# Loading a tile's rows from ScalarE's queue, and 159 tiles instead of 160, in a mixture-of-experts stage

## The reference

```python
B, S, H = (2, 512, 512)
E, G, TKG, K = (32, 8, 4, 8)
I, SI = (256, 512)
...
flat_idx = top_k_index.reshape(-1)
sort_idx = jnp.argsort(flat_idx)
xs = jnp.repeat(x, K, axis=0)[sort_idx]
group_sizes = jnp.bincount(flat_idx, length=E).astype(jnp.int32)
gate = jax.lax.ragged_dot(xs, w_gate, group_sizes)
up = jax.lax.ragged_dot(xs, w_up, group_sizes)
down = jax.lax.ragged_dot(jax.nn.silu(gate) * up, w_down, group_sizes)
unsort = jnp.argsort(sort_idx)
routed = (down[unsort].reshape(T, K, H) * tkw[..., None]).sum(axis=1)
```

## Time and profile before

| | |
|---|---|
| Median of 3 runs | 3160.15 us (3156.3 to 3161.93) |
| The profiled execution's own time | 3153.92 us |
| Its span, first to last instruction | 3151.8 us |
| Stage `expert_stage1` within it | about 2139 to 3152 us |
| TensorE clock granted, mean of the span | 0.961 of full speed |

### The profile page before, as it was taken

The page is one execution under the profiler, slowest core; times in us unless marked ns, Lnnn a source line. Parts: engine busy times, 40 slices in busy tenths (PEclk is TensorE's granted clock), DMA queues, the critical chain, the costliest instruction groups (busy, mean ns, idle before and its releaser), DMA issues. The chain is left out here.

```text
span 3151.8 us, 34237 instructions
## 1 busy us (share of the span) xinstructions
PE 2793.4 (89%) x9573; PEld 1264.9 (40%) x9574; DVE 1425.5 (45%) x2593; ACT 775.0 (25%) x1192; POOL 1211.3 (38%) x866
## 2 busy tenths in 40 slices
PE   5987975899999887689889988977999999999997
PEld 2343431344444343233333333433444454444453
DVE  7999999322000232376675646212332333232332
ACT  4746643200000010134333422001111111111111
POOL 2777656033000221154545321772333333333332
PEclk8999999999999998899999998988999999999999
DMA  3333221311200699730672002655656555756544
GB/s 123 118 101 101 81 66 48 111 55 56 71 14 38 230 354 327 200 100 1 170 196 68 1 1 92 262 223 147 149 125 147 127 130 129 182 127 149 125 89 72
DMA packets 270850, 386.49 MB, mean 123 GB/s; under 512 B 48546, under 2 KB 165091, under 8 KB 270754
## 3 DMA queue, kind: packets, MB, share of 16 engines
q1 hardware_dynamic: 212434, 243.23, 24.5%
q0 software_dynamic: 58320, 142.02, 19.1%
HBM read 237.38 MB, written 160.53 MB: 126 GB/s over the span
## 5 line engine op out<-in xcount | busy, mean ns | idle before, releaser
L1919 PE MATMUL e_psg<-e_wgu,e_xsT 128*128 x1280 | 592.7, 606 | 13.9 <-issue 8.9
L1799 POOL DMA_INDIRECT out_x<-e_yo,e_dest x160 | 255.7, 1598 | 637.5 <-DMA out_x<-e_yo,e_dest 452.9
L282 POOL TENSOR_TENSOR hc<-hs,bcst 128x1024 f32<-128x1024 f32 x128 | 300.6, 2349 | 178.4 <-DVE ps_b L502 171.4
L1919 PEld LDWEIGHTS e_psg<-e_wgu,e_xsT 128*128 128x128 f32 x1280 | 232.8, 192 | 258.5 <-issue 257.5
L627 PE MATMUL ps_y<-hc,ident 128*128 128x512 f32 x512 | 241.1, 609 | 90.4 <-POOL hc L282 90.1
L1868 DVE TENSOR_TENSOR e_h<-e_psg,e_sg 128x256 f32<-128x256 f32 x160 | 68.0, 425 | 530.4 <-ACT e_sg L1828 530.4
L1935 PE MATMUL e_pso<-e_wd,e_hT 128*128 x640 | 300.8, 592 | 0.7 <-DVE e_hT L1863 0.7
L508 DVE TENSOR_TENSOR_SCAN hs<-dA,ps_b 128x1024 f32<-128x1024 f32 x128 | 292.7, 2286 | 7.0 <-ACT dA L412 2.7
L1828 ACT ACTIVATE e_sg<-e_psg 128x256 f32<-128x256 f32 x160 | 61.3, 383 | 650.5 <-PE e_psg L1919 650.5
L1182 PE MATMUL r_ps_t<-r_wd,r_h 128*128 128x512 f32 x480 | 210.9, 600 | 10.3 <-issue 5.2
L412 ACT ACTIVATE dA<-dt,a_neg 128x511 f32<-128x511 f32 x256 | 165.6, 713 | 111.8 <-DVE hs L508 106.7
(11 more groups left out here) (404 smaller groups left out, 3861.7 us busy)
## 6 DMA issues: line engine op xcount, KB each, us to landing
e_xs<-slots_in POOLq DMA_DIRECT2D x160, 272.0 KB, 4.9
slots_in<-zeros SPq DMA_DIRECT2D x160, 256.0 KB, 2.3
bcst<-bc_rows SPq DMA_DIRECT2D x128, 256.0 KB, 4.3
e_wgu<-in_wg SPq DMA_DIRECT2D x32, 512.0 KB, 5.8
e_wgu<-in_wu SPq DMA_DIRECT2D x32, 512.0 KB, 7.0
e_wd<-in_wd SPq DMA_DIRECT2D x32, 512.0 KB, 7.9
e_w<-in_wg SPq DMA_DIRECT2D x11, 1408.0 KB, 15.5
e_w<-in_wu SPq DMA_DIRECT2D x11, 1408.0 KB, 16.8
```

What stands on the lines that cost most here:

```text
L282: pool.tensor_tensor(hc[:, it % 2, half(h), :], hs[:, it % 2, half(h), :], bc(bcst[:, q, 1, :], 1, HB), ALU.mult).then_inc(sem["hc"], 1)
L1799: pool.indirect_dma_start(out[:, :], bass.IndirectOffsetOnAxis(dest[:, q, 0:1], 0), yo[:, q, :], None, bounds_check=T + P - 1, oob_is_err= ...
L1919: j = pe.matmul(ps_g[:, q % 2, :], xsT[:, q % 2, k, :], wgu[:, bass.ds(e % RING, 1), k, :], start=k == 0, stop=k == KH - 1)
```

## The change

Three things change, all in or around `expert_stage1`.

1. The four first loads and all later ones (`load`, `reload`) move from POOL's program to ACT's. On ACT, `reload(t-1)` stands between `gate(t)` and `empty(t-1)`; on POOL only the adds are left.
2. `NTILE1` is worked out as (16384 + 32 x 127) // 128 = 159 instead of 16384 / 128 + 32 = 160. The slots in DRAM still number 160 x 128.
3. The last round of the loops has three tiles instead of four, and ACT's last round stands outside its loop.

```diff
-NTILE1 = T * K1 // P + E
-NSLOT1 = NTILE1 * P
+NTILE1 = (T * K1 + E * (P - 1)) // P
+NSLOT1 = (NTILE1 + 1) * P
...
-                def load(t, q):
-                    pool.dma_start(xs[:, q, :], D["xs1"][bass.ds(t * P, P), :]).then_inc(rows_in[q], 16)
...
-                def reload(t, q):
-                    hold(pool, sem["tr"], 1 + t + 1, c["held"])
-                    hold(pool, sem["dest"], 1 + t + 1, c["held"])
-                    load(t + RING, q)
...
                 with pool.Fori(1, ROUNDS - 1) as i:
                     for q in range(RING):
-                        reload(i * RING + q, q)
                         add(i * RING + q, q)
...
+                def load(t, q):
+                    act.dma_start(xs[:, q % RING, :], D["xs1"][bass.ds(t * P, P), :]).then_inc(rows_in[q % RING], 16)
+
+                def reload(t, q):
+                    hold(act, sem["tr"], 1 + t + 1, c["held"])
+                    hold(act, sem["dest"], 1 + t + 1, c["held"])
+                    load(t + RING, q)
...
-                with act.Fori(2, ROUNDS) as i:
+                with act.Fori(2, ROUNDS - 1) as i:
                     for q in range(RING):
                         gate(i * RING + q, q)
+                        reload(i * RING + q - 1, q + RING - 1)
                         empty(i * RING + q - 1, q + RING - 1)
```

More of the change, by code:

```diff
@@ L1730, in expert_stage1 @@
         RING = RING1
-        assert NTILE1 % RING == 0 and E % RING == 0
+        assert E % RING == 0
         assert AHEAD == RING - 1
@@ L1757, in expert_stage1 @@
         sem["out"] = pl.sem0("e1_out")
-        ROUNDS = NTILE1 // RING
+        ROUNDS = -(-NTILE1 // RING)
+        LAST = NTILE1 - (ROUNDS - 1) * RING
+        assert 1 < LAST < RING
         pl.start_at_one()
@@ L1801, in add @@
                         .then_inc(sem["out"], 16)
-                def reload(t, q):
-                    hold(pool, sem["tr"], 1 + t + 1, c["held"])
-                    hold(pool, sem["dest"], 1 + t + 1, c["held"])
-                    load(t + RING, q)
-                for q in range(RING):
-                    load(q, q)
-                reload(0, 0)
                 add(0, 0, first=True)
                 for q in range(1, RING):
-                    reload(q, q)
                     add(q, q)
@@ L1816, in _ @@
                     for q in range(RING):
-                        reload(i * RING + q, q)
                         add(i * RING + q, q)
-                for q in range(RING):
-                    add(NTILE1 - RING + q, q)
+                for t in range((ROUNDS - 1) * RING, NTILE1):
+                    add(t, t % RING)
                 pool.wait_ge(sem["out"], 16 * NTILE1)
@@ L1836, in empty @@
                        .then_inc(sem["yo"], 1)
+                def load(t, q):
[4 more added lines that the diff above has]
+                    load(t + RING, q)
+                for q in range(RING):
+                    load(q, q)
                 for t in range(RING):
@@ L1840, in _ @@
                     if t > 0:
+                        reload(t - 1, t - 1)
                         empty(t - 1, t - 1, first=True)
                 gate(RING, 0)
+                reload(RING - 1, RING - 1)
                 empty(RING - 1, RING - 1, first=True)
@@ L1845, in _ @@
                     gate(RING + q, q)
+                    reload(RING + q - 1, q - 1)
                     empty(RING + q - 1, q - 1)
-                with act.Fori(2, ROUNDS) as i:
+                with act.Fori(2, ROUNDS - 1) as i:
                     for q in range(RING):
                         gate(i * RING + q, q)
+                        reload(i * RING + q - 1, q + RING - 1)
                         empty(i * RING + q - 1, q + RING - 1)
-                empty(NTILE1 - 1, RING - 1)
+                for q in range(LAST):
+                    gate((ROUNDS - 1) * RING + q, q)
+                    if (ROUNDS - 1) * RING + q - 1 + RING < NTILE1:
+                        reload((ROUNDS - 1) * RING + q - 1, q + RING - 1)
+                    empty((ROUNDS - 1) * RING + q - 1, q + RING - 1)
+                empty(NTILE1 - 1, LAST - 1)
             @block.vector
@@ L1884, in a_round @@
                 def a_round(i, first=False, last=False):
-                    for q in range(RING):
+                    for q in range(LAST if last else RING):
                         t = i * RING + q
-                        if not (last and q == RING - 1):
+                        if not (last and q == LAST - 1):
                             turned_rows(t + 1, q + 1)
@@ L1903, in _ @@
                 a_round(ROUNDS - 1, last=True)
-                turned_hidden(NTILE1 - 1, RING - 1)
+                turned_hidden(NTILE1 - 1, LAST - 1)
             @block.tensor
@@ L1956, in _ @@
                 a_round(ROUNDS - 1, last=True)
-                turn_hidden(NTILE1 - 1, RING - 1)
-                down(NTILE1 - 1, RING - 1)
+                turn_hidden(NTILE1 - 1, LAST - 1)
+                down(NTILE1 - 1, LAST - 1)
 def attention_stage(nc, c, I, D, x, A, ln1, wr1, bias1):
```

## The result

The change ran in 3135.16 us (median of 4 executions, 3131.83 to 3141.76), the kernel before in 3159.53 us beside it: ratio 0.9933, 95% interval 0.9919 to 0.9948, 24.4 us faster. The forecast was 3165 us. Of the rivals, B with 3141 us came nearest. The profiled execution of the change is its slowest, 3141.76 us with a span of 3140.0; that of the kernel before is its fastest, so the two profiles lie only 11.8 us apart.

What follows compares the result with a forecast made beforehand. Adds were taken to bound the first stretch, PE the last. Terms -5.8 - 5 - 7 - 1 + 24 gave +5 us onto 3153.92, 3159; with the median 6 us above the profiled execution, 3165 us, range 3125 to 3195.

Steps and rivals of the forecast that it cites:

- B: Rival, faster: loads slip between the adds and cost them nothing; 3141 us, mostly 3125 to 3145; chance 0.30.
- What bounds the kernel: Last stage: adds, one at a time, pace the first stretch at 6.23 us, PE the second at 5.93 us.
- One tile, -5.8: Last stage: one padding tile fewer saves a quiet step of 5.68 to 5.93 us, taken as -5.8 us.
- Late rows, -5: First stretch: moving loads off POOL ends PE's 10.0 us of waits for rows; worth -5 us, between 0 and 10.0.
- tail, -7: Last 28 tiles: with PE entering in the lead, adds run at 5.68 instead of 5.93 us; -7 us at most.
- Start, -1: Stage start: the four first loads no longer wait for POOL's iotas; -1 us (0 to -3).
- ACT, 0: ACT's program: issuing a load takes 0.37 us, covered by 1.33 us of idle time between activations; cost 0.
- The load in the DMA engines, +24: DMA engines: a load ahead of an add's data delays it, 0.15 us a tile over 158 tiles, +24 us.
- Weights, 0 with 10 either way: Adds meeting weight loads: 28 meetings at 2.5 us each stay; 0, with 10 us either way.
- A: The forecast's own case: adds stay the bound, loads cost them 0.05 to 0.25 us; 3149 to 3181 us; chance 0.45.
- C: Rival, slower: loads collide with adds on most tiles, slower from 0.12 us per tile; 3188 to 3204 us; chance 0.20.
- D: Rival, slower: rows come late behind weights, PE stands 1.2 us after each of 28 triples; +15 us; chance 0.05.

Runs made afterwards that it cites:

- e6: The changed kernel with refills of three weight buffers in four bringing only 16 of 128 partitions; first stretch 5.96 us a step, no total time given.
- e7: The changed kernel with ScalarE's `reload` and `empty` swapped, so loads start later in a tile; its adds took 1003.4 us, no total time given.
- e8: 159 tiles, loads on GpSimd's queue one tile earlier, each of a refill's three weight transfers waiting for a further add to land; 0.9932 of the kernel before.
- e15: The changed kernel with refills in two steps, 1 MB at one add and 0.5 MB at the next, signalled behind the add's instruction; 0.988 of before.
- e13: e9 with the signal to SyncE from a small fill behind the add's instruction; 0.9925 of the kernel before.
- e3: The changed kernel once more, unaltered, for its spread and a second profile; 0.9966 of the kernel before.
- e12: The changed kernel once more, unaltered, beside the third group's runs on their chip; 0.9986 of the kernel before.
- e18: The changed kernel once more, unaltered, for comparison on the fifth group's chip; 3264.68 us, 0.9968 of the kernel before.
- e5: The changed kernel with loads bringing only the last 32 columns of the rows from tile 4 on; 0.9868 of the kernel before.
- e4: 159 tiles, loads on GpSimd's queue as in e1, but each reload a tile earlier; 0.9978 of the kernel before.
- e9: The changed kernel with each weight refill held until GpSimd's add of the expert's last tile, signalled by a queue increment; 1.0086 of the kernel before.
- e1: The kernel before with 159 tiles instead of 160, all loads still on GpSimd's queue; 0.9977 of the kernel before.

## Why the prediction was wrong

- **What bounds the kernel.** Right for the kernel before: adds in the first stretch, PE in the last.
- **One tile, -5.8.** Right within its error: 7.5 us, 4 to 11.
- **Late rows, -5; tail, -7.** PE's waits for rows are gone as said. The tail runs at 5.79 us and not at 5.68: 27 x 0.14 = 3.8 us. What the 5 were worth can't be told from the move as a whole.
- **Start, -1.** The first add starts 18.8 us after the first load, 20.3 before: 1.5 us. One gain wasn't in the sum: 2.0 us behind the last add (11.1 to 11.4 us in six traces with loads on GpSimd's queue, 9.1 to 9.6 in fourteen with loads on ScalarE's). The stage also begins 1.9 us sooner in the trace after, but that isn't shown to come from the change: in one group it began at 2239.9 us in `e6` and at 2248.1 in `e7`, both with loads on ScalarE's queue, and at 2246.1 in `e8` with loads on GpSimd's.
- **ACT, 0.** Right: where PE bounds the last stretch of `e15`, its step (tiles 130 to 157) is 5.90 us with the issue on ScalarE, 5.93 before.
- **The load in the DMA engines, +24.** This is the step that failed. The 0.15 us was fair as the price of a load's data: the runs give 0.09 to 0.13. (The 1.25 us it was built on is a stretch that moved 0.35 MB, not 272 KB; in `e13` a load's 272 KB took some 1.4 us, so little hung on it.) But I charged it on top of a quiet step of 5.68 us whose add already had a load behind it, so the old queue's price was in the base. What the change altered was the difference between the queues, and for quiet steps that end with a landing it is 0.02 us or nothing: 5.69 us before, 5.71 after; 5.82 to 5.84 in the first group. Without the 24, my sum gives 3141. That this lies 6 us from the measured 3135 is in part luck: by the ratios of `e3`, `e12` and `e18` the change would take 3149 to 3155.
- **Weights, 0 with 10 either way.** Right in size: +10.1 us in the profiled pair (+6.0 with each step counted once), +4.5 in the first group. But it was the term on which all hung. Refills go out at PE's beat, the adds lag it by an amount that shifts, and the place of each refill follows. From tile 24 to 129 an add starts 4.2 us after its `empty` on average before, 13.8 in the change (`e5` 7.2, `e7` 15.3), and 17 of 28 refills then stand at 3.15 us or more, 6 of 28 before. That PE, no longer stopped by late rows, makes this lag is the reading I find likely; no run moved the lag alone, and the lag isn't all: `e4`, loads on GpSimd's queue, lags 11.1 us and has 3 refills at 3.15 us or more. The sum also had no term for the queue of the rows at a meeting, where at 1.5 to 2.5 us the old one costs 1.1 us more; 11 of the 28 refills before stood there.

**The rivals.** B came nearest to the time, and its first half held: the loads cost the adds nothing more than before. The repeats, 3149 to 3155 us, fall into the low end of A (3149 to 3181). That 28 refills keep the adds over 6 us, which I held against it, is also true. C's mechanism exists, but the load is too small: its bound of 0.12 us per tile wasn't reached, as a difference between the queues. With 1.5 MB in the load's stead, ahead of an add's data at 27 of 28 refills (`e9`), the meeting costs 4 us. D didn't occur: rows landed in 2.8 us.

The forecast weighed a rule of the Trainium skill (DMA: Bandwidth & Descriptors, "Issuing engines are not separate DMA queues"): another issuing engine saves only issue time. For the quiet adds the runs agree (5.82 to 5.84 us), and by it alone the 24 us would have been 0. It doesn't cover order: rows behind an add on GpSimd's queue were late 16 times in `e1`, on ScalarE's in `e3` not once after the first.

**What stays open.** Why the kernel ends 2 us shorter with the loads on ScalarE's queue, and what sets the start of the stage: no row shows either. The spread of 43 us over the change's executions fits the place of the refills, since the versions that fix it spread 8 to 17 us over 4 to 6 executions, and `e7`, where nearly all stand late, 17 over 12; but `e4`, with free refills, spread only 10.0 us over 10, and only one execution of each run has a trace. The two change traces `e3` and `e18`, on two chips, lie 20 us apart: 10.0 of it is the start of the stage and 8.3 the adds. Why four executions of the change gave 0.9933 and 35 later ones 0.9966 to 0.9986 isn't known.

## What to carry to other kernels

A price for what is moved must be compared with the price at its old place; if the step from which one counts was measured with it in, only the difference is left. Where two streams of transfers meet and one of them is a chain that waits for each landing, ask not only how many bytes meet but when they start against a link of the chain: here the same 1.5 MB cost 4.1 us a meeting in `e9`, 2.3 in `e13` and, sent in two steps, 1.5 in `e15`. Tie the big, early transfers to a point behind the start of a link of the chain, and look in the trace whether the signal leaves where it is written.

## What the chip showed that I had not expected

- When the data starts decides most: weights ahead of an add left it 0.8% of the engines for 2 us (`e9`, 2614.4 to 2616.4), and then both moved, with 59.9% for the add. The Trainium skill (DMA: Bandwidth & Descriptors, "Queues, rings and completion order") has each engine turn between queues packet by packet; by that rule the add would have had about half from 2614.4 on. The first stretch doesn't agree, unless the add's packets weren't yet in its queue, which no row shows; the second does, roughly.
- Behind an increment written after GpSimd's indirect transfer, SyncE's issue came 0.03 us after that instruction's start; behind one hung on a small fill, 1.84 us after.
- Thinner rows made the meetings with *whole* weights cheaper by 31.6 us, about 22 of them, as an estimate, by shifting where the weights were issued.
